# Gram units of a DLRM-like recommendation MLP moved by a table of places, picks issued in other slots, layer 3 in another order, slice 14 padded

## The reference

```python
def _L0_rec_ref(bottom_output, W0, b0, W1, b1, W2, b2, W3, b3, W4, b4):
    b = bottom_output.shape[0]                       # 2048 samples, 27 inputs, 128 elements
    bottom_mlp_output = bottom_output[:, 0, :]
    interaction = jnp.einsum('bnd,bmd->bnm', bottom_output, bottom_output)
    interaction_flat = interaction[:, _TRIL_R, _TRIL_C]      # 351 pairs
    zero_pad = jnp.zeros((b, 1), bottom_output.dtype)
    x = jnp.concatenate([bottom_mlp_output, interaction_flat, zero_pad], axis=1)
    x = jax.nn.relu(x @ W0.T + b0)       # 480 -> 1024
    x = jax.nn.relu(x @ W1.T + b1)       # 1024 -> 1024
    x = jax.nn.relu(x @ W2.T + b2)       # 1024 -> 512
    x = jax.nn.relu(x @ W3.T + b3)       # 512 -> 256
    return x @ W4.T + b4                 # 256 -> 1
```

## Time and profile before

| what | us |
|---|---|
| median of 3 runs | 477.14 |
| lowest and highest | 476.85, 478.70 |
| profiled execution | 478.72 |
| its span | 476.9 |
| PE busy in the span | 447.3 |
| DVE, ACT busy | 253.1, 171.3 |
| mean granted share of PE's clock | 0.976 |

### The profile page before, as it was taken

How to read it: one execution, slowest core, us unless ns; L and a number is a source line. 1 busy time by engine, 2 the same in 40 slices (tenths; PEclk the granted TensorE clock), 3 DMA queues, 4 the chain that set the end, 5 groups by cost and what they waited for, 6 DMA issues and landing times.

```text
span 476.9 us, 13404 instructions
## 1 busy us (share of the span) xinstructions
PE 447.3 (94%) x5911; PEld 391.2 (82%) x5911; DVE 253.1 (53%) x498; ACT 171.3 (36%) x300; POOL 0.7 (0%) x6
## 2 busy tenths in 40 slices
PE   8998999899999996988998999799998999999996
PEld 8997987778887895877886878698997878999983
DVE  4886497457775575141435556624155657532344
ACT  3774352325344533130313354313032445211241
POOL 0000000000000000000000000000000000000000
PEclk9999899999999998898998999999999999999999
DMA  8968449977985359585872024978766000967400
GB/s 314 388 260 324 160 154 408 406 291 248 414 290 235 87 185 339 155 284 203 272 273 70 0 76 128 327 230 274 261 195 203 0 1 15 326 210 245 133 1 0
DMA packets 36779, 99.98 MB, mean 210 GB/s; under 512 B 3826, under 2 KB 5874, under 8 KB 35698
## 3 DMA queue, kind: packets, MB, share of 16 engines
q1 hardware_dynamic: 36722, 99.12, 59.4%
HBM read 82.33 MB, written 16.79 MB: 208 GB/s over the span
## 4 chain that ended last, share of the span: by engine, by line
PE 81%; DVE 6%; DMA 5%; issue 5%; SPq 2%; ACT 1%; ACTq 0%; DVEq 0%
PE work L1037 14%; PE work L1038 13%; PE work L1039 13%; PE acc L1037 7%; PE acc L1038 7%; PE acc L1039 7%; PE gps L1046 6%; PE gps L1037 3%; PE gps L1039 3%; PE gps L1038 3%; DMA xraw<-x_t 3%; DMA xmid<-x_t 2%; DVE turned L754 2%; PE gps L1087 1%; SPq L373 1%
## 5 line engine op out<-in xcount | busy, mean ns | idle before, releaser
L1039 PE MATMUL work<-featL,w0h 126*128 126x512 f32 (+5 forms) x160 | 56.2, 351 | 2.0 <-issue 2.0
L1037 PE MATMUL work<-featH,w0l 126*128 126x512 f32 (+5 forms) x160 | 57.8, 361 | 0.0
L1038 PE MATMUL work<-featH,w0h 126*128 126x512 f32 (+5 forms) x160 | 56.6, 354 | 0.0
L1037 PE MATMUL acc<-h2h,w2l 128*128 128x512 f32 x128 | 52.6, 411 | 0.0
L1038 PE MATMUL acc<-h2h,w2h 128*128 128x512 f32 x128 | 51.4, 402 | 0.7 <-issue 0.7
L1039 PE MATMUL acc<-h2l,w2h 128*128 128x512 f32 x128 | 50.9, 397 | 0.0
L1037 PE MATMUL work<-th,ring 128*128 128x256 f32 x144 | 41.8, 290 | 0.0
L1046 PEld LDWEIGHTS gps<-xraw 128*27 128x27 f32 x3136 | 29.6, 105 | 14.9 <-issue 12.8
L1038 PE MATMUL work<-th,ring 128*128 128x256 f32 x144 | 41.2, 286 | 0.0
L1039 PE MATMUL work<-tl,ring 128*128 128x256 f32 x144 | 41.2, 286 | 0.0
L1046 PE MATMUL gps<-xraw 128*27 128x27 f32 x3136 | 33.0, 193 | 8.4 <-issue 8.2
(11 more groups left out here) (124 smaller groups left out, 953.3 us busy)
## 6 DMA issues: line engine op xcount, KB each, us to landing
ring<-s_parts SPq DMA_DIRECT2D x48, 512.0 KB, 5.2
xraw<-x_t SPq DMA_DIRECT2D x50, 432.0 KB, 6.7
ring<-w_parts SPq DMA_DIRECT2D x36, 512.0 KB, 5.8
w_parts<-w1s SPq DMA_DIRECT2D x8, 1024.0 KB, 9.9
stage<-w_t SPq DMA_DIRECT2D x8, 512.0 KB, 8.0
s_parts<-sh SPq DMA_DIRECT2D x4, 1024.0 KB, 8.6
s_parts<-sl SPq DMA_DIRECT2D x4, 1024.0 KB, 10.8
xfirst<-x_t SPq DMA_DIRECT2D x9, 432.0 KB, 6.5
```

What stands on the lines that cost most here:

```text
L1037: pe.matmul(dst, wl, ah, start=start, stop=False)
L1038: pe.matmul(dst, wh, ah, start=False, stop=False)
L1039: return pe.matmul(dst, wh, al, start=False, stop=stop)
```

## The change

- **Units by a table.** `UNIT_PLACE` gives for each chunk the place of each unit: a block product, a step of layer 2, a tile of layer 0, the tile 0 of the next chunk (`NEXT`) or layer 3, and the step inside it. A unit can stand between two products of one accumulation. In chunk 1 three units stand in block products, and five near layers 3 and 0: unit 0 behind chunk 0's layer 3, and units 1 to 4 in chunk 1's layer 0. Chunk 2's are unit 0 behind `NEXT`, 1 behind layer 3, 2 to 4 in layer 0, 5 and 7 in blocks, 6 in layer 2. `UNIT_AT` and `TURN_AT` of chunk 0 are new too, and the unit ahead of its layer 0 is one of them now.
- **Picks sooner.** In chunks 1 and 2 quarter 0 is picked behind layer 0's tile 5 and turned in set 0. The later quarters follow a set sooner, and the last is picked between U4 and C11 of set 3 and turned at the same place as before.
- **Layer 3** goes over k first for the first half of k, for both tiles, and then tile by tile.
- **Slice 14** of chunk 0 takes the padded form.
- SP's loads of slices stand in other places; the x load of unit m+2 follows `keep_w1(m)`.

```diff
-FIRST_PADDED = [1, 2, 4, 5, 6, 8, 9, 10, 12]
+FIRST_PADDED = [1, 2, 4, 5, 6, 8, 9, 10, 12, 14]
...
-        UNIT_AT = {14: 1, 27: 2, 39: 3, 51: 4, 63: 5, 75: 6, 87: 7}
-        TURN_AT = {34: 0, 55: 1, 79: 2, 99: 3}
+        UNIT_AT = {20: 0, 31: 1, 40: 2, 58: 3, 65: 4, 79: 5, 98: 6, 105: 7}
+        TURN_AT = {48: 0, 71: 1, 91: 2, 113: 3}
...
-        UNIT_BEHIND = {3: 0, 5: 1}
+        UNIT_PLACE = [{("L3", 0, 0): 0},
+                      {("L0", 2, 1): 1, ("L0", 3, 3): 2, ("L0", 5, 1): 3, ("L0", 6, 3): 4, ("P3", 0, 3): 5, ("P1", 2, 3): 6,
+                       ("P5", 3, 3): 7, ("NEXT", 0, 0): 0, ("L3", 0, 0): 1},
+                      {("L0", 3, 3): 2, ("L0", 5, 2): 3, ("L0", 7, 0): 4, ("P5", 1, 3): 5, ("L2", 2, 0): 6,
+                       ("P6", 3, 3): 7}, {}]
+        LOADS_BEHIND = {(1, 1): 7, (2, 2): 8, (3, 2): 9}
...
+        def turned_sets(u):
+
+            return 0 if u < 5 else u - 4
...
                     keep_w1(m)
-                    for u in waits[m] if m != 1 else ():
-                        next_two(0, u)
+                    next_two(0, m + 2)
                     if m + 2 < MT1:
                         load_w1(m + 2)
...
                 if more:
-                    next_two(c, 2)
-                    next_two(c, 3)
+                    for u in range(2, 7):
+                        next_two(c, u)
...
             split_left(0)
             w0_lo_part(2)
+            pad_input(14)
...
                     second_of_two(c, k)
+                    if more and k == KQ - 2:
+                        pair_picks(c + 1, 0)
                 for i in range(SETS):
                     set_sum(c, i, "U2")
+                    set_sum(c, i, "U4")
+                    if more and i == SETS - 1:
+                        pair_picks(c + 1, i)
+                    set_sum(c, i, "C11")
+                    if more and i < SETS - 1:
+                        pairs_lo_part(c + 1, i)
+                    set_sum(c, i, "U3")
...
+            def unit_behind(c, name, n, step):
+
+                u = unit_of(c, name, n, step)
+                if u is not None:
+                    g = c + 2 if name in ("NEXT", "L3") else c + 1
+                    gram_unit(g, u, turned_sets(u))
...
                     last = product(place(i, name), ring[:, j, 0, cols], ring[:, j, 1, cols], *moving(k), k == 0, k == KQ - 1)
+                    if k < KQ - 1:
+                        unit_behind(c, name, i, k)
                 last.then_inc(block_done, 1)
+                unit_behind(c, name, i, KQ - 1)
...
-                    if more and i:
-                        transpose_pairs(c + 1, i - 1, 2 * i + 2)
+                    if more and i < SETS - 1:
+                        transpose_pairs(c + 1, i, i + 5)
                     p2(c, i)
                     if 0 < i < SETS - 1:
                         layer2_blocked(c, 2 * i - 1)
                     p7(c, i)
-                    if more and i < SETS - 1:
-                        gram_unit(c + 1, 2 * i + 2, i)
                     p4(c, i)
                     p3(c, i)
-                    if more and i < SETS - 1:
-                        gram_unit(c + 1, 2 * i + 3, i)
...
-                for k in range(KT3):
+                half = KT3 // 2
+                for k, m in [(k, m) for k in range(half) for m in range(MT3)] + \
+                        [(k, m) for m in range(MT3) for k in range(half, KT3)]:
                     if m == 0:
                         pe.wait_ge(split_done, nth(c, 2, k) + 1)
+                    if k == 0 and m:
+                        pe.wait_ge(relu_done, nth(c, 2, m) + 1)
```

More of the change, by code:

```diff
@@ L298, in unit_bank, with unit_of, units_in @@
             return gps[:, u % 2 if g == 1 else 0, :]
-        UNIT_BEHIND = {3: 0, 5: 1}
+        UNIT_PLACE = [{("L3", 0, 0): 0},
[4 rows of a table added]
+        LOADS_BEHIND = {(1, 1): 7, (2, 2): 8, (3, 2): 9}
+        def unit_of(c, name, n, step):
+            return UNIT_PLACE[c].get((name, n, step)) if isinstance(c, int) else None
+        def units_in(c, name, n, steps):
+            return [u for u in (unit_of(c, name, n, step) for step in steps) if u is not None]
+        def turned_sets(u):
+            return 0 if u < 5 else u - 4
         LEFT, RIGHT = slice(0, CHUNK // 2), slice(CHUNK // 2, CHUNK)
@@ L481, in body @@
                             load_block(c + 1, 0, j)
-                        units = {(0, 4): 4, (0, 6): 5, (1, 4): 6, (1, 6): 7, (2, 4): 8, (2, 6): 9}
-                        if more and (i, j) in units and (units[(i, j)] < UNITS or later):
-                            next_two(c, units[(i, j)])
+                        if more and (i, j) in LOADS_BEHIND and (LOADS_BEHIND[i, j] < UNITS or later):
+                            next_two(c, LOADS_BEHIND[i, j])
                         if (i, j) == (1, 2):
@@ L671, in layers @@
                 for m in range(EARLY, MT0):
+                    for u in units_in(c, "L0", m, range(KT0 - 1)):
+                        grams_from_psum(c + 1, u)
                     relu(c, 0, m, work[:, m % 2, :])
@@ L676, in layers @@
                         others_hi_part(c, m // 2)
-                    if more and m in UNIT_BEHIND:
-                        grams_from_psum(c + 1, UNIT_BEHIND[m])
+                    for u in units_in(c, "L0", m, [KT0 - 1]):
+                        grams_from_psum(c + 1, u)
                 for i in range(SETS):
@@ L701, in body @@
                     relu(c + 1, 0, 0, work[:, 0, :])
+                    for u in units_in(c, "NEXT", 0, [0]):
+                        grams_from_psum(c + 2, u)
                     t1_hi_part(c + 1, 0)
@@ L704, in body @@
                     relu(c, 3, m, acc[:, m, :], more)
+                for u in units_in(c, "L3", 0, [0]):
+                    grams_from_psum(c + 2, u)
                 if more:
@@ L1257, in layer3 @@
                                    k == 0, k == KT3 - 1)
-                last.then_inc(tile_done, 1)
+                    if k == KT3 - 1:
+                        last.then_inc(tile_done, 1)
             def layer4(c, more):
@@ L1337, in body @@
                     layer0(c + 1, 0)
+                    unit_behind(c, "NEXT", 0, 0)
                 if c == 0:
                     pe.wait_ge(w3_done, 1)
-                for m in range(MT3):
-                    layer3(c, m)
+                layer3(c)
+                unit_behind(c, "L3", 0, 0)
                 if more:
```

48 lines of the change are left out of this document (20 added, 28 removed).

## The result

The changed kernel takes **447.7 us** (median of 4 runs, 446.65 to 448.29); the kernel before took 477.0 in runs beside it (4 runs, 475.36 to 478.7). The ratio is 0.938, interval 0.934 to 0.942. In five more runs on another chip it was 447.62 (447.1 to 447.88). The forecast was 448.4. Between the profiled executions the gain is 478.72 - 448.29 = 30.4 us, which is also the difference of the spans, 476.9 - 446.5; the forecast was 28.7.

The account below looks back on a forecast made before the run. PE was taken as the bound, busy 447.3 of 476.9 us, so only its pauses and pace could give time: 32.8 us gained less 4.1 lost is 28.7, from 477.14 to 448.4 us, range 444.5 to 458.

Parts of the forecast that it names:

- units' places and the late load: PE's nine code pauses, 16.1 us, go but 2.5 remain; the pause behind a late x load gives 1.7 more.
- idle counted short: Twelve PE pauses, counted from the matmul's modelled end, each hide 0.16 us more idle time; gain 1.9 us.
- Part 1: Units' new places in PE's order: nine pauses at 256-instruction blocks go, gain 16.1 us, with 2.5 us of pauses remaining.
- Code is slower than I take it: Rival: every block of PE code takes at least 6.4 us, pauses 12.8 us instead of 2.5; 458.7 us, chance 0.10.
- The pauses are not of code: Rival: PE's pauses and slow clock, 16.1 and 7.6 us, stay; 470.9 us, chance 0.04.
- slower rival: Code comes at a steady 7.5 us per block, so 22 blocks of the new order pause; 487.4 us, chance 0.03.
- Part 2: PE's clock: without pauses of 2 us and more the five stretches at 1.2 GHz go; gain 7.6 us.
- Part 3: Earlier picks on DVE: PE's two waits of 2.1 us go and nothing new is late; gain 4.2 us.
- Part 4: Loads of slices start earlier, so the pause behind chunk 1's late x load goes; gain 1.7 us.
- Part 5: Layer 3 in chunk 3: tile 1's first products cover tile 0's wait for DVE's splits; gain 1.3 us.
- Part 6: Slice 14 of chunk 0 takes 2.00 us padded against 0.74 plain; cost 1.3 us.
- for what I miss: Allowance at slice 14, added to the cost of its padding; 0.3 us.

Follow-up runs that it names:

- e7: Changed kernel with the last quarter's picks back behind the splits of set 3; 452.48 us, 0.949 of the kernel before.
- e8: Changed kernel with layer 3's tiles one behind the other again; 449.07 us.
- e1: Changed kernel with 32 tiny float32 matmuls (128 PE instructions, half a block) of fill behind the warm-up transposes; 470.56 us, 0.982 of the kernel before.
- e2: Changed kernel with 64 tiny float32 matmuls (256 PE instructions, a whole block) of fill behind the warm-up transposes; 451.85 us, 0.942 of the kernel before.
- e3: Changed kernel with slice 14 plain again, which puts 96 more PE instructions there; 460.87 us, 0.960 of the kernel before.
- e9: Kernel before the change with 32 tiny float32 matmuls (128 PE instructions) of fill behind the warm-up; 478.26 us, 1.005 of the kernel before.
- e10: Changed kernel with two bursts of 192 tiny float32 matmuls (three blocks of 256 instructions each) in chunk 3; 473.33 us.
- e4: Changed kernel with DVE's dense parts of the next chunk moved back to the end of set 0; 446.72 us.
- e6: Changed kernel with DVE's dense parts back at set 0, the same kernel as e4 in another group; 446.67 us, 0.936 of the kernel before.
- e12: e1 with seven eighths of each x and ring load left out from slice 20 and set 1 of chunk 1 on; 460.0 us, 0.967.

## Why the prediction was right, and where it was not

| term | forecast, us | measured, us |
|---|---|---|
| units' places and the late load: pauses gone | 16.1 - 2.5 + 1.7 = 15.3 | 17.8 - 0.3 = 17.5 |
| clock | 7.6 | no stretch at 0.50 left |
| picks | 4.2 | 4.2 (e7 +4.9 with a slow stretch) |
| layer 3 | 1.3 | 1.0 in the trace (e8 1.45) |
| slice 14 | -1.3 - 0.3 | -1.0 |
| ring loads behind x0 | none | -1.3 |
| idle counted short | 1.9 | not measured by itself |
| sum | 28.7 | 29.9 with 7.6 and 1.9 taken over; the spans say 30.4, which leaves 10.0 for these two |

**Part 1** had the mechanism right, by counting in 256s: e1, e2 and e3 move the same work against the grid and bring back 17, 2 and 11 us of pauses. The failed step is the price of the pauses that remain, 2.5 us where 0.3 is measured. I sized it by the work of a block alone, from nine pauses of which six had stood beside a DMA share of 0.90 or more, from the entry to the start of the fetch. The new short blocks lie in layers 3 and 0, and in all but one of them the fetch starts 0.8 to 1.5 us behind the entry, so that a block of some 4 us is long enough. The three blocks of 4.1 to 4.8 that I priced at 1.2 us cost nothing; the one pause left, 0.3, stands behind a block of 5.4, beside a DMA share of 1.01 (above); the fetch started 3.4 us behind its entry. The same step made the expectations for e1, e3 and e9 too high. That only 3.2 us of work may be enough, and that a fetch may wait for 10 us, I did not have.

**Rivals.** "Code is slower than I take it" is out for these places: blocks of 5.3 us passed at full pace. It is true for single places: e1 needed 12.0 us for one block, at a DMA share of 0.94. "The pauses are not of code" is out by e1 and e2. What spoke against it beforehand, the counts of 256, held: the changed kernel has 46 packets of code, and its pause is on the same grid. The Trainium skill, "Runtime: NRT & Kernel Launch", section "Instruction fetch mechanics", calls the crossing into the next block mostly hidden. e10 agrees for a quiet DMA (two blocks of 3.2 us without a pause); e1 and the kernel before do not (4.3 and 3.6 us of idle), and there the measurement decides. The "steady 7.5 us" of the slower rival is out by the same rows.

**Part 2** came as forecast, by the rows: no pause for code over 0.3 us, clock 0.999. It was not measured by itself; e1, e3 and e7 show the price of its return only mixed with the waits.

**Part 3** was right in term and detail: C11 was not late, and nothing at P3 of set 3 or in layer 2 waits.

**Part 4** is the second failed step. Its gain came: no unit waits for x. But I went along SyncE's queue only for x slices, and did not ask what else in the queue depends on a step that the change moved. DVE's dense parts were moved by one set, the x0 load waits for them, and the ring loads stand behind it. That is a wait of 1.3 us in chunk 1; e4 and e6, without it, are 1.0 us faster.

**Part 5** was 0.3 too high by the trace: tile 0's first step is still slow (0.34 to the second product), and the last tile is followed by 0.36 before layer 4.

**Part 6** was 0.3 too high, and the 0.3 "for what I miss" did not come there. The misses cancel in part: 2.2 us more from the pauses and 0.6 less for the slice, against 1.3 for the ring and 0.3 for layer 3. That the sum came within 2 us of the spans is partly luck.

**Open.** The units' places alone, with everything else as before, were not run, and the old order was tried with one shift only (e9), so that another shift might help it too. Why a fetch waits 10 us in e1 and e12 at 65 us isn't known; the DMA share in these 10 us is 0.91 in e1, but most fetches at such shares started within 5 us. Nor is why the clock fell inside a burst in which PE's rows show no idle time.

## What to carry to other kernels

Short matmuls can outrun the delivery of their own code: look for idle time under "issue" that comes at multiples of 256 PE instructions (a matmul counts two with its weight load, a float32 one of few columns four, a wait one), and then spread the dense places over the entries, or shift them by half a block. A block needs some 3 to 4 us of work where DMA is quiet and mostly 4 to 6 where it is full, more at times (estimates: the starts of the fetches above and 2.2 to 2.7 us behind them), so put what is dense in instructions where transfers rest. Any edit that adds or removes PE instructions moves all that follows against the grid; if a small edit changes the time by 10 us or more, look there first. When a step moves on one engine, follow every queue that waits for it, and what stands behind that wait.

## What the runs showed of the hardware that was not expected

- 128 instructions of no use in front moved the time by 23 us; 256 by 4; 96 more at slice 14, in a form that is 1.0 us cheaper by itself, cost 13.
- From the start of a fetch to PE's entry it takes 2.2 us at the least, in all traces. From the entry to the start of the next fetch it was 1.0 us with DMA quiet and 2.6 with DMA full, as medians; the longest were 7 us and, at one place in e1 and e12, 9.9 (DMA share 0.91 in e1).
- The DMA queue shows a code packet as 0.9 to 2.1 us of transfer, so its share on the page (0.6 to 0.7%) says nothing about the harm it can do by being late.
- A burst of matmuls of 8 columns brought the granted clock to 0.50 for 6.8 us with no idle time in PE's rows (e10).
